# Neighbour sampling with one-hot picks: the one-hots of ranks two and three move to GpSimd

## The reference

```
mask = A != 0
scores = where(mask, -arange(N), -inf)
vals, idx = top_k(scores, 25)
agg = max over the valid idx of X[idx]
agg = where(degree <= 25, maximum(agg, 0), agg)
out = relu(concat([X, agg]) @ W + b)
y = layernorm(X + out)
```

## Time and profile before

| | |
|---|---|
| time, 3 runs | 752.6 us median, 746.86 to 757.48 |
| span of the profiled execution, first to last instruction | 755.6 us |
| busy DVE, PE, ACT, POOL | 644.0, 583.2, 482.6, 258.4 us |
| granted TensorE clock, mean | 0.920 |
| adjacency loads | 56 of 512 KB |

### The profile page before, as it was taken

One profiled execution on the slowest core, in us unless ns is written; L12 is line 12 of the kernel. 1 busy time (PEld: TensorE's weight loads), 2 busy tenths in 40 slices (PEclk: granted clock), 3 DMA queues, 4 the chain that ended last, 5 costly groups with the idle time before them and its releaser, 6 DMA issues.

```text
span 755.6 us, 13284 instructions
## 1 busy us (share of the span) xinstructions
PE 583.2 (77%) x3952; PEld 334.1 (44%) x3952; DVE 644.0 (85%) x916; ACT 482.6 (64%) x911; POOL 258.4 (34%) x309
## 2 busy tenths in 40 slices
PE   3768887988777877777877898778878878777863
PEld 2444544544444444444443555445434534444432
DVE  5887899989977689877897999989998867988894
ACT  6735775479646586556865688547965558644644
POOL 2324413454025440253402462236403534045500
PEclk9698999999889898998989999899998979999996
DMA  7611210322024220242202422142302411011102
GB/s 239 203 35 59 82 68 19 134 89 75 1 75 147 74 76 2 74 147 69 81 2 79 141 90 69 40 146 76 110 2 75 144 50 48 2 50 33 37 1 57
DMA packets 32674, 56.65 MB, mean 75 GB/s; under 512 B 4513, under 2 KB 21154, under 8 KB 32546
## 3 DMA queue, kind: packets, MB, share of 16 engines
q1 hardware_dynamic: 26146, 42.08, 16.6%
q0 software_dynamic: 6400, 13.12, 6.0%
HBM read 50.99 MB, written 4.19 MB: 73 GB/s over the span
## 4 chain that ended last, share of the span: by engine, by line
PE 32%; DVE 21%; issue 14%; DVEq 11%; ACT 11%; DMA 5%; another core or an unknown queue 4%; SPq 1%; ACTq 0%; POOL 0%; POOLq 0%
PE pair L939 21%; DVE part L683 9%; DVEq L753 6%; DMA adj_sb<-in_adj 5%; DVE hot L677 4%; DVE agg_t L776 3%; PE half L939 2%; PE misc L1001 2%; ACT maskT L480 2%; PE p_V L923 2%; DVEq L808 2%; PE misc L999 1%; DVE g_val L725 1%; ACT row_work L611 1%
## 5 line engine op out<-in xcount | busy, mean ns | idle before, releaser
L939 PE MATMUL pair<-hot,x_part 128*128 128x512 bf16 (+2 forms) x1608 | 388.5, 381 | 73.5 <-DVE part L683 48.3
L683 DVE TENSOR_REDUCE part<-pair 128x128 f32<-128x1024 f32 x256 | 311.1, 1218 | 85.1 <-PE pair L939 65.8
L939 PEld LDWEIGHTS pair<-hot,x_part 128*128 128x128 bf16 x1608 | 147.2, 101 | 240.6 <-issue 71.9
L397 POOL DMA_INDIRECT g_feat<-in_x,g_idx x200 | 191.3, 956 | 121.6 <-issue 95.3
L434 POOL TENSOR_TENSOR y_sb<-relu_sb,x_sb 128x128 f32<-128x128 f32 x64 | 30.0, 468 | 353.2 <-ACT relu_sb L539 353.0
L776 DVE TENSOR_REDUCE agg_t<-part 128x128 f32<-128x1024 f32 (+2 forms) x56 | 113.5, 2027 | 0.2 <-ACT part L546 0.2
L480 ACT ACTIVATE maskT<-p_maskT 128x1024 bf16<-128x1024 bf16 x56 | 57.0, 1018 | 51.1 <-PE p_maskT L911 24.7
L677 DVE TENSOR_SCALAR hot<-V 128x1024 bf16<-128x1024 bf16 x224 | 83.1, 384 | 0.0
L471 ACT ACTIVATE mask<-adj_sb 128x1024 bf16<-128x1024 int32 x56 | 58.9, 1053 | 34.5 <-DMA adj_sb<-in_adj 28.3
L546 ACT ACTIVATE part<-half 128x512 f32<-128x512 f32 x56 | 33.5, 598 | 68.0 <-PE half L939 57.1
L528 ACT ACTIVATE hot<-distance,one 128x1024 bf16<-128x1024 bf16 x56 | 64.2, 1146 | 0.1
(11 more groups left out here) (84 smaller groups left out, 616.6 us busy)
## 6 DMA issues: line engine op xcount, KB each, us to landing
adj_sb<-in_adj SPq DMA_DIRECT2D x56, 512.0 KB
g_adj<-in_adj SPq DMA_DIRECT2D x8, 512.0 KB, 4.2
x_sb<-in_x SPq DMA_DIRECT2D x8, 512.0 KB
out<-y_sb SPq DMA_DIRECT2D x7, 512.0 KB
g_feat<-in_x,g_idx POOLq DMA_INDIRECT x200
out<-y_sb SPq DMA_DIRECT2D x1, 448.0 KB
w_sb<-in_W SPq DMA_DIRECT2D x1, 128.0 KB
out<-y_sb SPq DMA_DIRECT2D x1, 64.0 KB
```

The costliest lines, as they stand in the source:

```text
L397: pool.indirect_dma_start(out=g_feat[w][:, k, :], out_offset=None, in_=x_rows, in_offset=bass.IndirectOffsetOnAxis(ap=g_idx[w][:, k:k + 1] ...
L683: dve.tensor_reduce(part[:, par(q, s), BANK + p], pairs[buffer_of(s, p)][:, :, :, :].rearrange("f a k i -> f i (a k)"), AX.X, ALU.max).the ...
L939: last = pe.matmul(dst, x_part[:, q, part_no, kb], one_hot, start=(part_no == 0), stop=(part_no == 2))
```

## The change

GpSimd makes the one-hots of ranks two and three, as comparisons of V with a constant, for every step. ACT's two passes for rank two go, with the array between them, and so does DVE's comparison for rank three; DVE starts at rank four, which shifts its remaining ranks among the gaps. POOL makes the one-hots of the step ahead as the first thing in a step, before the gathers, after the same two waits that the other engines have (V ready, and the buffer left by the step before). PE waits for ACT's rank one and POOL's ranks in place of ACT's rank two.

```diff
-ACT_RANKS = 2
+POOL_RANKS = (1, 2)
+DVE_RANK = 3
...
+            def one_hots(i, q, s):
+
+                m = pos(i, q, s)
+                wait(s_V, 2 * m + 2)
+                if not (isinstance(m, int) and m < 2):
+                    wait(s_half, m - 1)
+                for r in POOL_RANKS:
+                    last = pool.tensor_scalar(hot[:, par(q, s), r], V[:, q, s - 1], float(r + 1 - MARK), None,
+                                              ALU.is_equal)
+                last.then_inc(s_hotp, 1)
...
                 for s in range(1, NT):
+                    nxt = (i, q, s + 1) if s < MT else None if last else (ni, nq, 1)
+                    if nxt:
+                        one_hots(*nxt)
                     if s <= 5:
                         gather0(i, q, s)
...
             split_low(0, 0)
+            one_hots(0, 0, 1)
             run(pool, step)
...
-            def second_distance(i, q, s):
...
-            def second_rank(i, q, s):
...
                         first_rank(*nxt)
-                        second_distance(*nxt)
...
-                    if nxt:
-                        second_rank(*nxt)
...
-                    if r == ranks[0] == ACT_RANKS:
+                    if r == ranks[0] == DVE_RANK:
...
-                            one_hots(*nxt, range(ACT_RANKS + p, DEPTHS[nxt[2]][0], gaps), p == gaps - 1)
+                            one_hots(*nxt, range(DVE_RANK + p, DEPTHS[nxt[2]][0], gaps), p == gaps - 1)
...
-            one_hots(0, 0, 1, range(ACT_RANKS, DEPTHS[1][0]), True)
+            one_hots(0, 0, 1, range(DVE_RANK, DEPTHS[1][0]), True)
...
                     pe.wait_ge(s_hot, m + 1)
-                    pe.wait_ge(s_hot2, m + 1)
+                    pe.wait_ge(s_hot1, m + 1)
+                    pe.wait_ge(s_hotp, m + 1)
```

More of the change, by code:

```diff
@@ L91, in runs @@
         return list(zip(starts, starts[1:] + [NT]))
-    TABLES = 8 + sum(len(runs(DEPTHS[kind[0]])) for kind in KINDS)
+    TABLES = 6 + sum(len(runs(DEPTHS[kind[0]])) for kind in KINDS)
     x_rows = x.rearrange("b n c -> (b n) c")
@@ L116, in build @@
         first_bias = sb("first_bias", [P, 1], F32)
-        second_bias = sb("second_bias", [P, 1], F32)
-        one = sb("one", [P, 1], F32)
         falling = sb("falling", [P, N], F32)
@@ L137, in build @@
         hot_high = sb("hot_high", [P, 2, RANKS - LOW, HIGH_BLOCKS, P], BF16)
-        distance = sb("distance", [P, NT, P], BF16)
         hotx = sb("hotx", [P, DEEPER, NT, P], BF16)
@@ L220, in build @@
         s_hot1 = sem("first_rank_onehots_ready")
-        s_hot2 = sem("second_rank_onehots_ready")
-        s_distance = sem("distances_ready")
+        s_hotp = sem("pool_onehots_ready")
         s_std = sem("std_ready")
@@ L355, in _ @@
             pool.memset(first_bias[:, :], 2.0 - MARK).then_inc(s_tab, 1)
-            pool.memset(second_bias[:, :], MARK - 2.0).then_inc(s_tab, 1)
-            pool.memset(one[:, :], 1.0).then_inc(s_tab, 1)
             pool.wait_ge(s_ptab, 2)
@@ L649, in _ @@
             first_rank(0, 0, 1)
-            second_distance(0, 0, 1)
-            second_rank(0, 0, 1)
             run(act, step)
```

## The result

The changed kernel takes 796.6 us (median of 4 runs, 792.9 to 797.7), the kernel before 755.0 on the same chip: a ratio of 1.056, 95% interval 1.050 to 1.062. The forecast was 746, its range ended at 788. On a second chip, late in the study, the changed kernel came out at 796.7 again, while the kernel before had gone from some 757 to 787.6; the ratio there is 1.028, 1.020 to 1.036. Ratios in this document take the fast runs of a kernel alone, while 787.6 is the median of all 19 runs there, of which the fast ones took 769.5 to 779.0. So the change is slower on both, but how much slower hangs on the kernel before, whose time is the less steady one.

What follows compares the result with a forecast made beforehand. No single engine; DVE full in steps 4 and 5, ACT fullest in step 6. Savings 12 and 5 less holds 4, 5.6 and 1 give 6.4 us: 755.6 to 749.2, 746 against the median; eight in ten 728 to 788.

Steps and rivals of the forecast that it cites:

- What bounds the kernel: In one undisturbed batch, no engine bounds everywhere: DVE is full in steps 4 and 5, ACT fullest in step 6.
- What DVE saves: One 1024-column comparison fewer in each of 56 steps: 12 us, between 6.7 and 18.5.
- What ACT saves: Two passes fewer in 56 steps, mostly beside waiting: 5 us, mainly in step 6, between 2.7 and 22.
- What POOL pays: Two comparisons of 128 x 1024 a step, each 1.2 us, between 0.99 and about 2.4.
- Where POOL's work lies: Comparisons begin at the half bank; POOL's later work moves back 2.4 us, so it enters step 6 about 4 us late.
- What DVE loses: DVE held by POOL: 4 us in step 6, 5.6 at batch ends, 1 at the start of the first step.
- The forecast's rule: A DVE comparison that meets a POOL tensor operation is held to the end of that operation.
- The sum: Savings less holds come to 6.4 us: 749.2 from the profiled span, 746 against the median, 0.9% less.
- The rivals: Three other cases: POOL's comparison dear (0.27), ACT's relief worth its upper end (0.23), POOL's one-hots too late (0.05).
- The dear comparison: POOL's comparison takes 1.6 us or more: 769 at 1.6, above 800 at 2.4, PE waiting in step 6; chance 0.27.
- The sign named for being wrong: Comparison of 1.6 us or more, DVE held in steps 4 and 5 too, or PE waiting for POOL.
- Late queue: POOL's one-hots, behind the residual's wait for ACT or the levels, come too late though cheap: 768; chance 0.05.

## Why the prediction was wrong, step by step

- **What bounds the kernel.** The steps were read rightly, DVE full in 4 and 5. But the batch was chosen as undisturbed, and so 22 us of stalls in the steps 3 of four other batches (15.6 to 17.1 us long) never came into view.
- **What DVE saves**, taken as 12. The relief of ACT alone gives 736.5, with DVE's comparison gone too 726.0: 10.5 us, or 13 by the ratios (0.973 to 0.955), across two chips. As far as that goes, right.
- **What ACT saves**, taken as 5. Measured nothing (734.2 and 736.5). What stood ahead of the half copies only waits longer: ACT's wait for the half bank is 62.8 us in the run with the wait alone and 111.3 with the relief added. The lower end, 2.7, was the better reading.
- **What POOL pays**, taken as 1.2. This step failed. It is 2.78, above the upper end of 2.4 too. The single-input row nearest in kind had only 56 columns, and by the prices above more than half of its 369 ns is fixed time, so the slope had to come from another row, and I took it from the iota, which reads nothing. The row that reads 1024 columns, the subtraction, was nearer in what matters, and I set it aside as dearer because it has two inputs. The Trainium skill's loop (GPSIMD Engine Reference, section 7, Performance pitfalls), quoted in the forecast at 2.03 or 1.03 cycles an element, is not what this comparison does: at the forecast's 1.2 GHz 2.5 ns are 3 cycles, and an addition costs the same.
- **Where POOL's work lies.** The reckoning was right and the number in it wrong. With 5.5 us in place of 2.4, POOL's steps 3 to 5 are 3.1 us longer each, and its comparisons start some 7 us late in step 6 in the mean (4 forecast), 12 in batch five. The reckoning also put the gathers that move back at nothing, as they "are reduced only at the end of step 6". That failed both ways: a start up to 3 us later gained 21 us, and gathers that run on into the half bank have ACT wait for PE's late signals.
- **What DVE loses.** Forecast 4 in step 6, 5.6 at the batch ends, 1 at the start. At the forecast's price the whole change of time is 3, not 10.6. At the real one the holds are mostly in steps 4, 5 and 6 (15.9, 17.5 and 27.2 us), and step 7, where the batch ends lie, became shorter. The forecast's rule, that a comparison is held to the end of POOL's operation, fits its one row, a two-input subtraction, but not POOL's comparisons: in the changed kernel eleven of DVE's comparisons that began early in one ended 1.31 to 1.34 us into it, about half-way.
- **The sum.** With the forecast's price really paid, 384 columns, the kernel takes 728.9. The forecast's profile-based 749.2 less the unseen 22 of step 3 would be 727. So two errors stood against each other: a gain of 22 that was not seen, and a loss of 70 where 10.6 was charged. Its own range is not what its ends give either: gains of 9 to 30 against holds of 3 to 25 are 726 to 769 from the median, not 737 to 766.
- **The rivals.** The dear comparison was the case that came, with its place (step 6), its point of decision (1.6 us) and, at 2.4, its time ("above 800") nearly right. It had PE wait for POOL 44 us there. The waits name POOL for 3.4 only. What grew in their place are PE's waits for DVE's reductions, from 48.3 to 73.0 us, and ACT's for half banks that are signalled late, from 8.2 to 43.2. The sign named for being wrong, a comparison of 1.6 us or more, and DVE held in steps 4 and 5, both showed.
- **Late queue.** It had little chance for the reason that the residual ends in time; with 5.5 us in each step that reason fell.

Left open: why PE's signals come late while POOL's gathers run; and how much of the loss is due to them, to DVE's holds and to POOL's late one-hots, since a late comparison makes all three.

## What to carry to other kernels

Price an instruction that is moved to another engine from a row of that engine that reads as much, not from one that does the same operation on little or one that only writes; where none does both, the dearest neighbour is no upper end. Add up what the receiving engine does per step and compare it with the step: as long as the sum fitted, the work was nearly free here (3 us with 384 columns), and when it exceeded the step by some 2 us the delay grew from step to step. An engine that is late also moves its other work, here the gathers, to an hour at which it disturbs others. And look at the steps of all batches before one is called typical.

## What the runs showed of the hardware

- POOL's one-input comparison of 128 x 1024 takes 2.77 us, 2.5 ns a column, more than its two-input subtraction of as many (2.11).
- DVE instructions that meet POOL's are held: the comparison of 128 x 128 took 412 ns in the mean (219 before), the reciprocal of 8 columns 1.48 us and the two-input multiplication behind it 0.89 in the rows above. The Trainium skill (SBUF — State Buffer, Who interferes with whom) lets the first holder of the shared port pair keep it for the whole instruction. The trace agrees that the comparison and the multiplication are held, but not that it is for the whole instruction: the comparison that ended at 481.09 got through 1.34 us into a POOL comparison that began at 479.75 and lasts 2.78.
- While POOL's gathers run, signals of PE come up to 4.7 us behind the recorded ends of their matmuls: 152 in the kernel before, 102 in the changed one, none in the run without gathers.
- Gathers that start up to 3 us later made the kernel 3% faster, without any work removed.
- After waits of 3.4 and 5.8 us PE's next matmuls ran at a granted clock of 0.50, so each wait cost about 1.3 us more than its length.
